# Attention masks added to the scores by eight 64x64 identity products on TensorE's quarters instead of four 128x128 ones

## The chip, the cores and the metric

One core of one Trainium2 chip runs the whole program. The metric is device time in microseconds (us) of one execution, as the median of several runs. TensorE multiplies matrices (PE in the profile; PEld is its loading of weights, which overlaps the multiplying), VectorE is DVE, ScalarE is ACT, GpSimd is POOL, and SyncE (SP) issues most DMAs.

## What is computed

A batch of 32 sequences of 128 tokens, 128 channels wide, passes through attention, a mixture of experts, attention with rotary positions, and a second mixture of experts, each with a layer norm before it and a sum with its input after it. Both attentions have 16 heads of 8 channels and read 77 keys from a context of their own. The change touches only the masking of their scores:

```python
# first attention: one mask for all sequences (128 x 77), one of padding for each sequence (32 x 77)
scores = jnp.einsum('bqhd,bkhd->bhqk', q, k) * SCALE
scores = jnp.where(attn_mask[None, None, :, :], -jnp.inf, scores)
scores = jnp.where(key_padding_mask[:, None, None, :], -jnp.inf, scores)
attn = jax.nn.softmax(scores, axis=-1)
# second attention: a query sees the 65 keys up to its own position
idx = q_pos + jnp.arange(-64, 1)[None, :]
local_mask = (idx < 0) | (idx >= S_k)
```

## The kernel before

Each attention is a pipeline over the 32 sequences, written out by hand: every engine has its own list of instructions, and semaphores tie the lists together. For sequence k TensorE does, in this order: turn the output of sequence k-2 (L1373), make the scores of k (`scores`, L1318), turn the shifted scores of k-1 so that keys lie on partitions (L1348, L1351), turn rows (L1382 to L1388), multiply by the values of k-1 (L1365), and make projections and router logits (L1416 to L1424). VectorE takes the maximum of each head's scores (L1061), subtracts it (L1062), and between these does the layer norm's statistics, the router and the sums with the input. ScalarE takes the exponentials and copies PSUM banks (a bank is a part of the accumulators) to SBUF. GpSimd spreads the keys of later sequences ahead of time (`keys`, L551), prepares values and sends token rows to the experts with indirect DMAs (L620).

The scores of one sequence fill four banks of the tile `S`, one for each group g of four heads: 128 queries on the partitions, 4 x 77 = 308 columns. `scores` waits until the query projection has been taken (`products_taken` or `q_set`), until the keys are spread (`kexp_ready`), and until VectorE has read the scores before (`sub_done`). Then it issues four products of 32 rows by 128 columns in float32 (L1328), each on its own quarter of TensorE's rows and into its own bank. The profile shows two matmul records for each of them, as for every float32 product. Four products of the 128x128 identity in bf16 with the masks then add the masks into the same four banks (L1330). The mask is one 128x77 tile read four times over. The last of the four raises `s_ready`, on which L1061 waits.

The masks come from two places. In the first attention GpSimd adds, for each sequence, the common mask `negA` and that sequence's padding `negP` into a ring `bias_qk` of 13 slots (L561), ahead of TensorE by up to 13 sequences. `negA` is made once by VectorE (L1139) from bytes that SP loads (L438). In the second attention the mask is one tile `bandb`, copied once by GpSimd (L532) from the constants `cst`, while the experts of the first half still run. Those constants come in one load behind the first few (L2200), which SP issues before the moves of the values (L709) and the loads behind them.

Of the kernel before, what the change touches and what calls it, by code (L numbers as in the profile page):

```python
# [13 lines left out]
U8 = mybir.dt.uint8  # L14
# [36 lines left out]
C_QUARTER = 716  # L51
C_END = 730
# [10 lines left out]
WARM = 38  # L63
CHUNK_AT = ((0, 128), (488, 360))

def shape_constants():
# [5 lines left out]
    c[:, C_BAND:C_BAND + TK] = np.where((k < q - WINDOW) | (k > q), MASKED, 0.0)  # L73
    half = DH // 2
# [175 lines left out]
def attention(nc, st, layer, w):  # L250
# [43 lines left out]
    if rope:  # L294
# [6 lines left out]
        bandb = sb("bandb", [128, TK], BF16)  # L301
    else:
# [3 lines left out]
        bias_qk = sb("bias_qk", [128, KR, TK], BF16)  # L306
        am8 = sb("am8", [128, TK], U8)
        negA = sb("negA", [128, TK])
# [126 lines left out]
    def sync(sp):  # L435
        if not rope:
            sp.dma_start(pad8[:, 0:SOON], w["pad"][:, 0:SOON]).then_inc(masks_in, 16)
            sp.dma_start(am8[:, :], w["am"]).then_inc(masks_in, 16)  # L438
# [78 lines left out]
    def gpsimd(pool):  # L517
        steps = Steps(pool_step)
        zero = st["zero"]
        if not rope:  # L520

            nc.gpsimd.memset(mv[:, :, :, :], 1.0).then_inc(mv_set, 1)
            nc.gpsimd.memset(raw[:, 2 * G:3 * G, :, :], 0.0).then_inc(mv_set, 1)
            nc.gpsimd.memset(vm[:, :, :, :], 0.0)
            nc.gpsimd.memset(xn[:, :, 0:1], 1.0)
            nc.gpsimd.memset(onesb[:, :], 1.0).then_inc(mv_set, 1)
            pool.wait_ge(mv_set, 3)
            pool.wait_ge(st["cst_in"], 48)
        else:
            pool.wait_ge(consts_in, n_const)  # L530
            pool.wait_ge(st["consts_in"], st["n_consts"])
            nc.gpsimd.tensor_copy(bandb[:, :], cst[:, C_BAND:C_BAND + TK]).then_inc(masks_set, 1)  # L532
# [18 lines left out]
        def keys(n):  # L551
# [7 lines left out]
            if not rope:  # L559
                pool.wait_ge(masks_set, 1 if n < MOVED_FIRST else 3)  # L560
                steps.mark(nc.gpsimd.tensor_tensor(  # L561
                    bias_qk[:, n % KR, :], negA[:, :], negP[:, n * TK:(n + 1) * TK], ALU.add))
# [341 lines left out]
    def vector(dve):  # L904
# [232 lines left out]
        if not rope:  # L1137
            dve.wait_ge(masks_in, 48)
            V.tensor_scalar(negA[:, :], am8[:, :], MASKED, None, ALU.mult)  # L1139
# [177 lines left out]
    def tensor(pe):  # L1317
        def scores(n):  # L1318
# [6 lines left out]
            masks = bandb[:, :] if rope else bias_qk[:, n % KR, :]  # L1325
            for g in range(G):
                heads = slice(32 * g, 32 * g + 32)
                nc.tensor.matmul(S[:, g, 0:GK], qT[heads, n % 2, :], kexp[heads, n % KR, :, :], start=True, stop=False)  # L1328
            for g in range(G):
                last = nc.tensor.matmul(S[:, g, 0:GK], identb[:, :], masks.unsqueeze(1).broadcast_to([128, J, TK]),  # L1330
                                        start=False, stop=True)
# [117 lines left out]
        else:  # L1449
# [3 lines left out]
            pe.wait_ge(masks_set, 1)  # L1453
# [873 lines left out]
def layout(v):  # L2327
# [17 lines left out]
    out["a0_am"], out["a0_amT"], out["a0_pad"], out["a0_padT"] = mask, mask.T, np.repeat(pad.reshape(1, -1), 128, 0), pad.T  # L2345
# [44 lines left out]
```

## Time and profile before

| what | us |
|---|---|
| median of 3 runs | 703.93 |
| lowest and highest run | 702.35, 705.06 |
| span of the profiled execution | 699.0 |
| median less that span | 4.93 |
| TensorE busy in the span | 653.6 |
| VectorE busy | 527.0 |
| GpSimd busy | 507.5 |
| ScalarE busy | 421.3 |

The profiled execution's own time outside its span is not given by the profile, so the difference of 4.93 us between median and span stands for what lies around the span. The attentions fill about 14 to 190 us and 366 to 548 us of the span. TensorE's granted clock is at the full 2.4 GHz in nearly all of both; at half of it (1.2 GHz) only in a few short stretches, of which one covers the start of the second attention. Busy times of TensorE are modelled, and a busy engine isn't always the one that sets the pace: the chain of waits and the idle times of the other engines decide that.

### The profile page before, as it was taken

Reading aid. Unit: us, or ns where it says so; the run is one execution under the profiler, and the core shown is the slowest. Engines: PE = TensorE matmul, PEld = TensorE weight load, DVE = VectorE, ACT = ScalarE, POOL = GpSimd, SP = SyncE. Lnnn points to the kernel's source line nnn. Section 1 sums busy time; section 2 is a strip of 40 time slices with the busy share of each in tenths; the row PEclk is TensorE's granted clock in tenths of the full one; section 3 lists DMA queues with packets and bytes.
Section 4 is the critical chain, followed back from the end, with each engine's and each line's share of the span. In section 5 each row is a group of like instructions: output and inputs, shape, how many; then the busy total and the mean of one; then the engine's idle time right before and its main releaser. Section 6 shows DMA issues by size and latency. Waiting matters only on the chain.

```text
span 699.0 us, 20550 instructions
## 1 busy us (share of the span) xinstructions
PE 653.6 (94%) x6836; PEld 550.9 (79%) x6836; DVE 527.0 (75%) x1507; ACT 421.3 (60%) x1166; POOL 507.5 (73%) x844
## 2 busy tenths in 40 slices
PE   8899999999988999999988999999899787999998
PEld 6577777777766999999985777777676676999997
DVE  4589999999853566665445789999999578778876
ACT  5567777776545333333444667677674675777773
POOL 5865588668765898887767776888787776777671
PEclk9999999999989999999997999999999999999999
DMA  5490001011423332334311101011121013333375
GB/s 178 112 352 6 10 26 33 26 33 35 159 68 93 116 119 62 95 97 126 88 41 35 32 17 32 29 59 46 35 71 49 32 48 98 103 100 101 94 251 195
DMA packets 45404, 57.69 MB, mean 83 GB/s; under 512 B 11379, under 2 KB 37142, under 8 KB 44630
## 3 DMA queue, kind: packets, MB, share of 16 engines
q1 hardware_dynamic: 36086, 38.12, 18.4%
q0 software_dynamic: 8640, 17.97, 7.6%
q8 instruction: 58, 0.95, 0.6%
q10 hardware_dynamic: 576, 0.29, 0.2%
q14 instruction: 44, 0.36, 0.2%
HBM read 33.77 MB, written 22.08 MB: 80 GB/s over the span
## 4 chain that ended last, share of the span: by engine, by line
PE 38%; DVE 23%; POOL 20%; issue 11%; DMA 2%; ACT 2%; SPq 2%; DVEq 0%; POOLq 0%; ACTq 0%
POOL results L1624 10%; PE S L2059 6%; PE ptp L2078 6%; DVE mx L1061 5%; DVE pr L1062 5%; PE M L1365 4%; PE S L1328 4%; POOL rows L620 3%; PE ptp L1348 3%; PE S L1330 3%; POOL xi L1617 3%; PE M L1416 2%; PE S L2065 2%; PE ptp L1351 2%; SPq L709 1%
## 5 line engine op out<-in xcount | busy, mean ns | idle before, releaser
L620 POOL DMA_INDIRECT rows<-out_rows,posi x128 | 126.9, 991 | 48.5 <-issue 28.5
L803 ACT ACTIVATE pT<-ptp 128x512 f32<-128x512 f32 (+1 forms) x192 | 94.1, 524 | 79.4 <-PE ptp L1348 72.3
L1061 DVE TENSOR_REDUCE mx<-S 128x16 f32<-128x1232 f32 x64 | 91.2, 1425 | 16.4 <-PE S L1330 15.8
L1624 POOL DMA_INDIRECT results<-early,xi x71 | 74.8, 1053 | 31.3 <-DVE early L1688 24.1
L1062 DVE TENSOR_TENSOR pr<-S,mx 128x1232 f32<-128x1232 f32 x64 | 92.2, 1441 | 2.2
L1929 POOL DMA_INDIRECT results<-early,xs x71 | 69.2, 975 | 27.4 <-issue 17.1
L1714 PE MATMUL S<-early,w1s 128*128 128x128 f32 x568 | 77.6, 280 | 5.0 <-DVE w1s L1681 3.3
L1724 PE MATMUL S<-first_w,early 128*128 x568 | 75.6, 276 | 0.7 <-DVE early L1688 0.7
L1714 PEld LDWEIGHTS S<-early,w1s 128*128 128x128 f32 x568 | 70.3, 195 | 7.6 <-issue 6.1
L1660 ACT ACTIVATE early<-S 128x128 f32<-128x128 f32 x71 | 19.6, 276 | 84.3 <-PE S L1707 84.3
L1688 DVE TENSOR_SCALAR early<-S,xs 128x128 f32<-128x128 f32 x71 | 24.9, 350 | 60.0 <-PE S L1724 33.2
L1365 PE MATMUL M<-pT,vm 128*32 128x128 f32 (+1 forms) x2048 | 70.0, 277 | 0.0
L1724 PEld LDWEIGHTS S<-first_w,early 128*128 128x128 f32 x568 | 69.0, 192 | 1.2 <-issue 0.9
L1348 PE MATMUL ptp<-cst,pr 128*128 128x128 f32 x512 | 68.9, 279 | 0.1
L1348 PEld LDWEIGHTS ptp<-cst,pr 128*128 128x128 f32 x512 | 61.7, 145 | 2.8 <-DVE pr L1062 0.3
L1328 PE MATMUL S<-first_w,qT 32*128 32x308 f32 x512 | 52.3, 477 | 11.0 <-DVE pr L1062 3.5
L1365 PEld LDWEIGHTS M<-pT,vm 128*32 128x32 f32 (+1 forms) x2048 | 52.4, 110 | 12.1 <-issue 11.6
L2059 PE MATMUL S<-early,w1s 128*128 128x128 f32 x426 | 53.7, 276 | 3.7 <-DVE w1s L1982 3.7
L2078 PE MATMUL ptp<-W,kT 128*128 (+1 forms) x412 | 56.3, 278 | 0.0
L2059 PEld LDWEIGHTS S<-early,w1s 128*128 128x128 f32 x426 | 50.4, 192 | 4.3 <-issue 4.3
L2078 PEld LDWEIGHTS ptp<-W,kT 128*128 128x128 f32 x412 | 52.2, 194 | 0.6
L1681 DVE COPY w1s<-first_w 128x512 f32 x71 | 39.9, 562 | 12.7 <-PE S L1714 7.8
(222 smaller groups left out, 1556.5 us busy)
## 6 DMA issues: line engine op xcount, KB each, us to landing
xs<-rows SPq DMA_DIRECT2D x142, 66.0 KB, 1.8
first_w<-in_e_W SPq DMA_DIRECT2D x2, 2048.0 KB, 8.5
swap<-results SPq DMA_DIRECT2D x32, 128.0 KB
first_w<-results SPq DMA_DIRECT2D x6, 512.0 KB, 7.9
rows<-out_rows,posi POOLq DMA_INDIRECT x128, 2.3
x_res<-in_x SPq DMA_DIRECT2D x1, 1536.0 KB, 8.6
W1r<-in_e_W SPq DMA_DIRECT2D x1, 1536.0 KB, 10.9
out_x<-x_res SPq DMA_DIRECT2D x3, 512.0 KB, 3.8
```

The lines of the kernel that those rows point to most:

```text
L620: nc.gpsimd.indirect_dma_start(rows[:, :], bass.IndirectOffsetOnAxis(posi[:, k, n:n + 1], 0), out_rows[:, ring_slot(groups, n), k, :], Non ...
L803: nc.scalar.activation(pT[0:rows_of, G * r:G * r + count, :], ptp[q % 2][0:rows_of, 0:count, :], ACT.Exp, scale=SCALE)\
L1061: do(V.tensor_reduce(mx[:, :].rearrange("p (g j) -> p g j", g=G), sc, AX.X, ALU.max))
L1062: V.tensor_tensor(pr[:, n % 2, :, :].rearrange("p (g j) k -> p g j k", g=G), sc, mx[:, :].rearrange("p (g j) -> p g j", g=G).unsqueeze(3). ...
L1328: nc.tensor.matmul(S[:, g, 0:GK], qT[heads, n % 2, :], kexp[heads, n % KR, :, :], start=True, stop=False)
L1348: last = nc.tensor.transpose(ptp[q % 2][:, g, :], flat[:, g // 2, at:at + 128], ident)
L1365: last = nc.tensor.matmul(OT[32 * g:32 * g + 32, half * T:(half + 1) * T], vm[0:rows_of, n % 2, block + g, :], pT[0:rows_of, chunk, :], st ...
L1624: nc.gpsimd.indirect_dma_start(results[:, :], bass.IndirectOffsetOnAxis(xi[:, s:s + 1], 0), ys[:, s, :], None)\
L1714: last = nc.tensor.matmul(hTp[n % 2][:, c, :], w1s[:, n % 2, c * 128:(c + 1) * 128], xsT[:, n % 3, :], start=True, stop=True)
L1724: last = nc.tensor.matmul(yp, hT[:, n % 2, c, :], w2[:, c, :], start=(c == 0), stop=(c == FC - 1))
L2059: last = nc.tensor.matmul(out[:, at * 128:(at + 1) * 128], w1s[:, u % 2, at, c * 128:(c + 1) * 128], xsT[:, r % 3, at, :], start=True, sto ...
L2078: last = nc.tensor.matmul(yp(u)[:, at, :], hT[:, u % 2, c * 256 + at * 128:c * 256 + (at + 1) * 128], w2[:, c, :], start=(c == 0), stop=(c ...
```

## The change

The four full mask products of a sequence become eight of 64 rows by 64 columns. Each uses one of the four quarters of TensorE: the rows (partitions of identity and mask) are the lower or the upper 64, the columns (partitions of `S` that are written) too. Banks 0 and 2 take their masks from the two quarters on the diagonal, banks 1 and 3 from the other two. For those two the mask has to lie on the opposite half of the partitions, so every mask is kept twice, the second time with its two halves exchanged (`np.roll` by 64). That doubles `bandb`, `bias_qk`, `negA` and the bytes `am8`, adds 77 columns to the constants, a second copy on GpSimd in the second attention, and makes the sum L561 twice as wide. The score products now close their accumulation (`stop=True`), and the mask products add onto them. TensorE's second attention waits for both copies.

```diff
-C_QUARTER = 716
-C_END = 730
+C_SWAP = 716
+C_QUARTER = 793
+C_END = 807
+MASKS_AT = [(g + odd, rows_at, 64 - rows_at if odd else rows_at) for g in (0, 2) for odd in range(2) for rows_at in (0, 64)]
+    c[:, C_SWAP:C_SWAP + TK] = np.roll(c[:, C_BAND:C_BAND + TK], 64, 0)
-        bandb = sb("bandb", [128, TK], BF16)
+        bandb = sb("bandb", [128, 2, TK], BF16)
-        bias_qk = sb("bias_qk", [128, KR, TK], BF16)
-        am8 = sb("am8", [128, TK], U8)
-        negA = sb("negA", [128, TK])
+        bias_qk = sb("bias_qk", [128, KR, 2, TK], BF16)
+        am8 = sb("am8", [128, 2, TK], U8)
+        negA = sb("negA", [128, 2, TK])
-            nc.gpsimd.tensor_copy(bandb[:, :], cst[:, C_BAND:C_BAND + TK]).then_inc(masks_set, 1)
+            nc.gpsimd.tensor_copy(bandb[:, 0, :], cst[:, C_BAND:C_BAND + TK]).then_inc(masks_set, 1)
+            nc.gpsimd.tensor_copy(bandb[:, 1, :], cst[:, C_SWAP:C_SWAP + TK]).then_inc(masks_set, 1)
                 steps.mark(nc.gpsimd.tensor_tensor(
-                    bias_qk[:, n % KR, :], negA[:, :], negP[:, n * TK:(n + 1) * TK], ALU.add))
+                    bias_qk[:, n % KR, :, :], negA[:, :, :], negP[:, n * TK:(n + 1) * TK].unsqueeze(1).broadcast_to([128, 2, TK]), ALU.add))
-            V.tensor_scalar(negA[:, :], am8[:, :], MASKED, None, ALU.mult)
+            V.tensor_scalar(negA[:, :, :], am8[:, :, :], MASKED, None, ALU.mult)
-            masks = bandb[:, :] if rope else bias_qk[:, n % KR, :]
+            masks = bandb[:, :, :] if rope else bias_qk[:, n % KR, :, :]
             for g in range(G):
                 heads = slice(32 * g, 32 * g + 32)
-                nc.tensor.matmul(S[:, g, 0:GK], qT[heads, n % 2, :], kexp[heads, n % KR, :, :], start=True, stop=False)
-            for g in range(G):
-                last = nc.tensor.matmul(S[:, g, 0:GK], identb[:, :], masks.unsqueeze(1).broadcast_to([128, J, TK]),
-                                        start=False, stop=True)
+                nc.tensor.matmul(S[:, g, 0:GK], qT[heads, n % 2, :], kexp[heads, n % KR, :, :], start=True, stop=True,
+                                 skip_group_check=True)
+            for g, rows_at, q_at in MASKS_AT:
+                rows_of, q_of = slice(rows_at, rows_at + 64), slice(q_at, q_at + 64)
+                last = nc.tensor.matmul(S[q_of, g, 0:GK], identb[rows_of, rows_of],
+                                        masks[rows_of, int(rows_at != q_at), :].unsqueeze(1).broadcast_to([64, J, TK]),
+                                        start=False, stop=True, skip_group_check=True)
-            pe.wait_ge(masks_set, 1)
+            pe.wait_ge(masks_set, 2)
-    out["a0_am"], out["a0_amT"], out["a0_pad"], out["a0_padT"] = mask, mask.T, np.repeat(pad.reshape(1, -1), 128, 0), pad.T
+    out["a0_am"], out["a0_amT"], out["a0_pad"], out["a0_padT"] = np.stack([mask, np.roll(mask, 64, 0)], 1), mask.T, np.repeat(pad.reshape(1, -1), 128, 0), pad.T
```

## Rows read from the trace of the kernel before

**Rows 1.** The page: its span, and part 4, the chain that ended last.

```profile
span 699.0 us, 20550 instructions
...
PE 38%; DVE 23%; POOL 20%; issue 11%; DMA 2%; ACT 2%; SPq 2%; DVEq 0%; POOLq 0%; ACTq 0%
POOL results L1624 10%; PE S L2059 6%; PE ptp L2078 6%; DVE mx L1061 5%; DVE pr L1062 5%; PE M L1365 4%; PE S L1328 4%; POOL rows L620 3%; PE ptp L1348 3%; PE S L1330 3%; POOL xi L1617 3%; PE M L1416 2%; PE S L2065 2%; PE ptp L1351 2%; SPq L709 1%
```

**Rows 2.** Busy time by stretch: us, PE, PEld, DVE, ACT, POOL, clock, DMA share, GB/s.

```profile
32.00:64.00 32.00, 31.90 (x407) 23.85 (x404) 27.04 (x58) 22.48 (x66) 19.95 (x49) 1.00 0.61 231
64.00:98.00 34.00, 33.85 (x457) 25.49 (x457) 32.07 (x86) 25.76 (x74) 22.79 (x48) 1.00 0.04 14
98.00:142.00 44.00, 42.72 (x553) 32.29 (x550) 41.97 (x124) 31.47 (x91) 34.89 (x64) 1.00 0.09 28
142.00:190.00 48.00, 45.94 (x615) 34.46 (x617) 45.59 (x145) 31.39 (x84) 36.07 (x62) 1.00 0.21 71
366.00:396.00 30.00, 25.94 (x276) 18.49 (x277) 18.61 (x28) 15.32 (x44) 21.52 (x44) 0.83 0.11 33
396.00:450.00 54.00, 53.87 (x690) 41.04 (x693) 46.99 (x112) 39.41 (x123) 40.01 (x83) 1.00 0.10 29
450.00:548.00 98.00, 91.14 (x1162) 68.60 (x1154) 89.77 (x273) 61.76 (x184) 77.83 (x138) 0.98 0.17 49
```

**Rows 3.** Chains of the stretches, in order of time: start, us, what (groups of pieces).

```profile
32.13 0.64 PE S L1330 x4
32.77 0.87 PE ptp L1348 x8
...
77.50 0.67 PE S L1330 x4
...
78.19 1.45 DVE mx L1061
...
508.93 0.64 PE S L1330 x4
```

**Rows 4.** Timeline of one sequence's scores, narrow windows: start, us, engine, line, count.

```profile
92.30 0.20 PEld L1328 LDWEIGHTS S<-first_w,qT 32*128 32x128 f32 x4
...
92.19 0.54 PE L1328 MATMUL S<-first_w,qT 32*128 32x308 f32 x4
...
92.56 0.44 PE L1328 MATMUL S<-first_w,qT 32*128 32x308 f32 x4
...
92.92 0.10 PEld L1330 LDWEIGHTS S<-bias_qk,identb 128*128 128x128 bf16 x1 [0.42 <-issue]
...
93.08 0.57 PE L1330 MATMUL S<-bias_qk,identb 128*128 128x308 bf16 x3
...
93.49 0.27 PE L1348 MATMUL ptp<-cst,pr 128*128 128x128 f32 x1
```

**Rows 5.** Timeline of the value products on quarters of 32 columns, same sequence.

```profile
95.13 1.08 PE L1365 MATMUL M<-pT,vm 128*32 128x128 f32 x32
...
95.15 0.25 PEld L1365 LDWEIGHTS M<-pT,vm 128*32 128x32 f32 x9
```

**Rows 6.** The waits: weight loads before the masks in the run; VectorE from 98 to 142 us.

```profile
PEld S L1330 <- issue: 27.6, 64, 0.8
...
DVE mx L1061 <- PE S L1330: 0.3, 1, 0.3
```

**Rows 7.** Single lines that the change widens or repeats: ns min/median/max, first and last start.

```profile
L561 POOL TENSOR_TENSOR bias_qk<-negA,swap x32: 312/326/347, 9.1 to 121.4; 128x77 bf16<-128x77 f32 x32
...
L563 POOL TENSOR_TENSOR first_w<-kT,cst x64: 693/702/716, 9.3 to 450.2; 128x308 f32<-128x308 f32 x64
...
L1139 DVE TENSOR_SCALAR negA<-am x1: 202/202/202, 6.9 to 6.9; 128x77 f32<-128x77 uint8 x1
...
L532 POOL CAST bandb<-cst x1: 257/257/257, 333.9 to 333.9; 128x77 bf16<-128x77 f32 x1
```

**Rows 8.** DMA issues by line: count, KB each, us to landing.

```profile
cst<-in_cst SPq DMA_DIRECT2D x1, 275.0 KB, 6.0
```

More of the change, by code:

```diff
@@ L437, in sync @@
             sp.dma_start(pad8[:, 0:SOON], w["pad"][:, 0:SOON]).then_inc(masks_in, 16)
-            sp.dma_start(am8[:, :], w["am"]).then_inc(masks_in, 16)
+            sp.dma_start(am8[:, :, :], w["am"]).then_inc(masks_in, 16)
             sp.dma_start(ctxT[:, SOON:], st["ctxT_dram"][:, SOON:]).then_inc(ctx_in[1], 16)
```

## The prediction

> **What bounds the kernel now.** I read the page first. The chain that ended last spends 38% on TensorE, 23% on VectorE and 20% on GpSimd, and the mask products L1330 alone are 3% of the span of 699.0 us, some 21 us [rows 1]. The 64 blocks of 0.64 us are 41 us, so about half of them lie on the chain. So the second view was the busy time by stretch, to see who sets the pace where. From 32 to 64 and from 396 to 450 us TensorE has no idle time (31.90 of 32, 53.87 of 54) while VectorE has 5 and 7 us to spare. From 64 to 142 us VectorE is nearly as full as TensorE (32.07 of 34, 41.97 of 44), from 142 to 190 us it stays so, and from 450 to 548 us TensorE, VectorE and GpSimd are each idle for some of the 98 us (6.9, 8.2 and 20.2), so they wait for one another [rows 2]. The third view, the chain of each stretch in order of time, tells what a shorter mask block is worth. I counted the L1330 blocks on it, and what follows each [rows 3]: 32 of 64 blocks lie on it, from the one at 32.13 us to the one at 508.93 us. After 26 of them the chain stays on TensorE (as at 32.13, with the transposes L1348 behind), after 6 it goes over to VectorE's maximum (as at 77.50, with L1061 at 78.19). The 26 gain what the block gets shorter for TensorE, the 6 what `s_ready` comes earlier. By stretch (TensorE next, VectorE next): 32 to 64 us 7 and 0; 64 to 98 2 and 2; 98 to 142 3 and 2; 142 to 190 none; 366 to 396 4 and 1; 396 to 450 8 and 0; 450 to 548 2 and 1.
>
> **The block itself, now.** In the timeline of one sequence the weight load of the first mask product starts at 92.92 after an idle time of 0.42 that no semaphore ended ("issue"), and the matmul of L1348 starts at 93.49: the block is 0.57 us [rows 4]. Three products after the first one take (93.49 - 93.08) / 3 = 0.137 each; the first has 0.16. So 308 columns of bf16 stream in 0.137, and the load of a full identity hides but for some 0.02.
>
> What the idle 0.42 is matters most. The second half of the score products starts at 92.56. The two halves are 92.56 - 92.19 = 0.37 apart, of which 92.30 - 92.19 = 0.11 is the load of 128 columns (the second loads go out when the first are in), so 0.26 is streaming. The last score product has streamed by about 92.84 (0.02 for its place as fourth), and the mask load waits for another 0.08 to 0.09, and isn't pulled ahead of it, as the load of L1348 is under the mask products. 
> - Load of 64 columns. The nearest rows are 0.11 for 128 columns (above) and 95.15 - 95.13 = 0.02 to 0.03 for 32 [rows 4, 5]. By columns 64 lie at 0.055; bounds 0.03 and 0.11. The second four loads hide under the first four products, as in both those rows.
> - Streaming. Four row quarters run side by side in L1328, and four column quarters side by side in L1365, there into one bank: 32 products in 1.08 us, where L1348 takes 0.87 for eight with as many columns [rows 3 to 5]. So I take two rounds of four at 0.137, 0.27, and 0.02 for the places in the round.
> - The way out. The array is in quarters before and whole after, so what came for nothing now costs a drain, 0.09 as at 92.84, and an open load for L1348, between 0.03 and 0.11, taken as 0.07. Lower bound: nothing of the 0.16, if the load is pulled ahead as before. Upper bound: 0.20.
>
> Sum: 0.055 + 0.27 + 0.02 + 0.09 + 0.07 = 0.51 against 0.57: TensorE gains 0.06 a sequence, with bounds of a gain of 0.24 (0.03 + 0.27 + 0.02 = 0.32) and a loss of 0.05 (0.11 + 0.27 + 0.02 + 0.11 + 0.11 = 0.62). Halving the products is mostly paid back on the way out. For VectorE more is left: the last mask product starts 0.43 after the first load now (93.49 less one product, 93.35, against 92.92) and 0.055 + 0.137 + 0.02 = 0.21 after it then, so `s_ready` comes 0.22 earlier (bounds 0.16 and 0.24).
>
> The page TensorEngine Tiling (Array Packing) of the Trainium skill states, under Key Properties, that changing the tiling mode drains the engine. The way in shows it here, as an idle 0.42; no row shows the way out. By that rule the lower bound, and with it the first rival below, falls away.
>
> **Along the chain.** 32 to 64 us: 7 x 0.06 = 0.42. 64 to 98: 2 x 0.06 + 2 x 0.22 = 0.56, of the 1.9 that VectorE has free. 98 to 142: 3 x 0.06 + 2 x 0.22 = 0.62, but VectorE waits there for scores for only 0.3 in all [rows 6], and its list is the same, so 0.3. 142 to 190: VectorE is late, not TensorE; 0. 366 to 396: 4 x 0.06 + 0.22 = 0.46. 396 to 450: 8 x 0.06 = 0.48. 450 to 548: VectorE is busy for 89.77 of 98 and GpSimd for 77.83, with the scatters L620 in its queue [rows 2]; I count nothing there, and I take half of the 0.94 of the second attention as given back in it, because those scatters keep their own pace. That is 0.42 + 0.56 + 0.3 + 0.47 = 1.75.
>
> **What it adds.** L561 gets 154 columns for 77: GpSimd took 326 ns for 77 and 702 ns for 308 (L563), so 154 are at 0.45, 0.12 more (at most 0.33, doubled) [rows 7]. That is 4 us over 32 sequences on an engine with 11 to 12 us free from 32 to 64 and from 64 to 98 us each [rows 2], up to 13 sequences ahead; the sums end at 121.4 us, and the indirect DMAs queued behind them in GpSimd's list have that slack too. If it had none, 4 us would show. Cost 0. L1139 on VectorE is on the path of the start, before the first values are moved: between 0 and 0.20 more, taken as 0.1. The second copy of the band mask, 0.26, stands in GpSimd's queue at 334 us between indirect DMAs of the experts; GpSimd waits for VectorE behind it, so 0, at most 0.26. TensorE's wait for it is 30 us later: 0. The constants grow by 77 x 128 x 4 bytes = 38.5 KB of 275, at 6.0 us for all: at most 0.8 if they were alone on the path, taken as 0.1, since the value moves behind them on SP wait for VectorE [rows 7, 8]. Together 0.2.
>
> So 1.75 - 0.2 = 1.55 us. Off the profiled execution that is 699.0 - 1.55 = 697.45 of span; with the 4.93 between span and median, 702.4.
>
> **The rivals.**
> - *No way out to pay.* If the load of L1348 is pulled ahead out of the quarters, TensorE gains 0.24: 1.7 from 32 to 64, 1.0 from 64 to 98 (VectorE waits there, all told, no more than 1.0 to 1.9), 0.3, then half of 12 x 0.24 + 0.25 = 3.1, so 1.55, less 0.2: 4.35 us, 699.6. For it: L1348's load was hidden before. Against it: L1330's load wasn't, at the same kind of border, in any of 64 sequences [rows 4, 6].
> - *Two row halves in one bank take turns (slower).* Each bank now gets its lower and its upper queries from two different row halves. Nothing in the trace has that: L1328 gives each row quarter its own bank, and L1365's column quarters, which share one, all use the full rows. If such a pair can't write side by side, the eight run as first; second and third; fourth and fifth; sixth and seventh; eighth: five steps for two. The block is 0.055 + 0.69 + 0.02 + 0.16 = 0.92, 0.35 longer than now, and `s_ready` comes 0.19 later. On the chain 26 x 0.35 + 6 x 0.19 = 10.2; from 142 to 190 us TensorE has 2.1 free against 9 x 0.35 = 3.2, so 1.1 more, and 0.7 at the borders of other stretches: 12 us, 715.9. It decides from the first step beyond four: at four the block is no longer shorter. The same page of the Trainium skill, under Gotcha 1: PSUM Pressure, says that different row tiles can't use one PSUM bank at the same time; taken by the letter it gives this case. L1365 speaks against it in part: quarters that write other partitions of one bank run side by side.
> - *No two quarters run together.* Eight times 0.137: 0.76 longer a sequence, 64 x 0.76 = 49 less what TensorE has free in rows 2 outside the chain, some 12: 37 us, 741.
> - *The four small loads queue up.* 4 x 0.055 ahead of the first round: the block is 0.1 longer than now, `s_ready` 0.06 to 0.1 earlier: 26 x 0.1 less 6 x 0.08, 2.1 us, 706. Against it: four loads of L1328 go out within 0.02 [rows 4].
>
> **How the numbers follow.** Chances: the forecast 0.60, no way out to pay 0.14, turns in a bank 0.14, queued loads 0.08, none together 0.04. The likeliest is 702.4, its own range 700.5 to 705. The range of 8 in 10 takes in the first rival and the queued loads and leaves out the two slow ones (0.18): 698.8 to 707.5. About 0.5%, 3.5 us, is what a measurement of this kernel can tell from no change, below 700.4 or above 707.4. Faster: most of the first rival and a little of the forecast, 0.17. Slower: 0.19. Within: 0.64.
>
> **What would show it.** In the profile after: the weight loads before the masks still idle for about 0.4; four mask matmuls start within 0.03 and the next four 0.14 later; an idle time before the load of L1348 that wasn't there, and 0.50 from the first mask load to L1348. VectorE's waits for the scores nearly vanish between 64 and 142 us, L1061 and L1062 stay at 1.4 us, L561 is at 0.45. Two starts 0.14 apart within one four would show turns in a bank. The forecast is wrong if the way out costs nothing, or more than 0.22.

## The result, and the profile after

The changed kernel takes 700.17 us (median of 8 runs, 697.25 to 703.74) where the kernel before, on the same chip, takes 704.62 (8 runs, 701.84 to 707.39): a ratio of 0.9935, with a 95% interval of 0.9907 to 0.9963. Two repeats beside other kernels gave 698.62 and 697.41 us, ratios 0.9939 and 0.9943. So the kernel is 4.5 us faster by this first comparison, and somewhere between 2.6 and 6.6; the forecast was 1.55 us off the span, and 702.4.

The runs of one kernel differ by several microseconds, and most of that goes with the mean granted clock in each run's record: over 201 runs of all kernels of this study, a microsecond more at the lower clock (1.2 GHz) is 0.35 us more of time. Where "clock taken out" stands below, this straight line is taken off. Slow executions are left out: three of before (711, 741 and 2137 us) and one of the copies alone (709 us). For the three rows of the change together (32 runs, against 82 of before) it leaves -3.4 us, with a 95% interval of 0.4. The mean time at the lower clock is 28.4 us in these rows and 29.6 in before, no clear difference, so the gain isn't a matter of the clock.

First the page of the changed kernel: its span, the chain that ended last by engine, and two of the costliest groups (busy time, mean ns of one, idle time just before and what ended it).

```profile
span 697.7 us, 21063 instructions
...
PE 34%; POOL 23%; DVE 22%; issue 13%; DMA 3%; ACT 2%; SPq 2%; POOLq 0%; DVEq 0%; ACTq 0%
...
L1065 DVE TENSOR_REDUCE mx<-S 128x16 f32<-128x1232 f32 x64 | 91.1, 1424 | 11.8 <-PE S L1336 11.6
...
L1355 PEld LDWEIGHTS ptp<-cst,pr 128*128 128x128 f32 x512 | 57.1, 145 | 16.2 <-issue 15.8
```

The lines have moved: the scores L1328 are L1332, the masks L1330 are L1336, the transposes L1348 are L1355, the maximum L1061 is L1065, the sums L561 are L565. On the chain TensorE falls from 38% to 34% [rows 1]. The last line is the new one: the weight loads of the transposes now idle for 15.8 us that no semaphore ended, some 0.25 before each sequence's first.

The busy time by stretch, with the columns of [rows 2]:

```profile
32.00:64.00 32.00, 31.43 (x435) 21.92 (x435) 26.80 (x59) 23.16 (x73) 22.42 (x51) 1.00 0.65 241
64.00:98.00 34.00, 33.63 (x484) 24.50 (x486) 32.65 (x85) 25.91 (x74) 23.59 (x49) 1.00 0.05 15
98.00:142.00 44.00, 41.62 (x586) 29.61 (x586) 42.45 (x125) 31.96 (x92) 35.88 (x65) 1.00 0.08 26
396.00:450.00 54.00, 53.62 (x741) 38.97 (x738) 47.49 (x114) 39.49 (x122) 40.66 (x83) 1.00 0.10 29
450.00:548.00 98.00, 89.86 (x1224) 65.19 (x1223) 89.52 (x279) 62.50 (x185) 77.36 (x138) 0.98 0.17 50
```

From 64 to 142 us VectorE is fuller than before (32.65 and 42.45 us for 32.07 and 41.97) and TensorE less so, GpSimd is busy for 0.8 to 1.0 us more in each of the two stretches, and in the second attention TensorE is still full from 396 to 450 [rows 2].

Then one sequence's scores, in narrow windows of the timeline of TensorE and its weight loads, the counterpart of [rows 4] (a window shows what runs in it, so a count depends on where the window is set).

```profile
92.88 0.44 PE L1332 MATMUL S<-first_w,qT 32*128 32x308 f32 x4
...
93.24 0.11 PEld L1336 LDWEIGHTS S<-bias_qk,identb 64*64 64x64 bf16 x4 [0.42 <-issue]
...
93.24 0.33 PE L1336 MATMUL S<-bias_qk,identb 64*64 64x308 bf16 x4
...
93.40 0.31 PE L1336 MATMUL S<-bias_qk,identb 64*64 64x308 bf16 x4
...
93.64 0.20 PEld L1355 LDWEIGHTS ptp<-cst,pr 128*128 128x128 f32 x2 [0.25 <-issue]
...
93.70 0.14 PEld L1355 LDWEIGHTS ptp<-cst,pr 128*128 128x128 f32 x1
```

The second half of the scores starts at 92.88, the first mask load at 93.24, after the same idle 0.42 as before. Four mask products start together at 93.24, four more at 93.40; the first load of the transposes waits until 93.64, and when it is in, at 93.70, the next one goes out. From the first mask load to that point the block takes 0.46 us, where 0.57 stood before (92.92 to 93.49, where the transposes' first weights were already in) [rows 4]. The last mask product starts 0.18 after the first load, where it started 0.43 after it. The sequence of [rows 4] is one of the longer ones of before: over 61 blocks the median is 0.545 before and 0.456 after, so 0.09 is the gain of a typical sequence, and 0.11 that of the longer form.

### The profile page after: what moved, and what is told of

It is laid out like the page before. It is cut to its first block, busy times and chain, and to the rows that moved or that the text cites. A ratio compares the mean times of both kernels' runs of the same rounds, so it can differ in the third digit from the quotient of the medians.

```text
span 697.7 us, 21063 instructions
## 1 busy us (share of the span) xinstructions
PE 648.6 (93%) x7092; PEld 535.8 (77%) x7092; DVE 527.4 (76%) x1507; ACT 421.5 (60%) x1166; POOL 514.5 (74%) x845
## 4 chain that ended last, share of the span: by engine, by line
PE 34%; POOL 23%; DVE 22%; issue 13%; DMA 3%; ACT 2%; SPq 2%; POOLq 0%; DVEq 0%; ACTq 0%
POOL results L1631 9%; PE S L2066 6%; PE ptp L2085 6%; POOL rows L624 5%; DVE mx L1065 5%; DVE pr L1066 5%; PE M L1372 4%; PE ptp L1355 3%; PE S L1332 3%; POOL xi L1624 3%; POOL rstd L552 2%; PE S L1336 2%; PE S L2072 2%; SPq L713 1%; PE M L1423 1%
## 5 line engine op out<-in xcount | busy, mean ns | idle before, releaser
L1065 DVE TENSOR_REDUCE mx<-S 128x16 f32<-128x1232 f32 x64 | 91.1, 1424 | 11.8 <-PE S L1336 11.6
L1355 PE MATMUL ptp<-cst,pr 128*128 128x128 f32 x512 | 72.1, 285 | 0.1
L1355 PEld LDWEIGHTS ptp<-cst,pr 128*128 128x128 f32 x512 | 57.1, 145 | 16.2 <-issue 15.8
L1332 PE MATMUL S<-first_w,qT 32*128 32x308 f32 x512 | 53.1, 484 | 11.5 <-DVE pr L1066 4.2
```

What stands on the lines that cost most here:

```text
L1065: do(V.tensor_reduce(mx[:, :].rearrange("p (g j) -> p g j", g=G), sc, AX.X, ALU.max))
L1355: last = nc.tensor.transpose(ptp[q % 2][:, g, :], flat[:, g // 2, at:at + 128], ident)
```

## The experiments

Two theories of the change go through the expectations. **P**: the price per block, multiplied along the chain as the prediction did it, with the block that the trace of after shows (0.11 us for TensorE, 0.25 for the scores), is what the kernel gains; its rivals are that a good part is given back later, and that products in one bank or one quarter hold one another up. **G**: GpSimd's wider sums, priced at nothing, cost part of the first attention.

The traces are compared by the starts of VectorE's 64 maxima, one for each sequence. Two profiles of the kernel before (the second is the last experiment but one) show which stretches repeat: from maximum 4 to 12, 12 to 20, 20 to 31, 40 to 47 and 47 to 60 they agree within 0.11 us, so differences there are the kernel's. Elsewhere they don't: 1.2 us apart from 0 to 4, 0.5 from 31 to 32 (the experts lie between), 0.8 from 32 to 40 and from 60 to 63, and 3.2 after the last. The table gives each stretch less that of the first profile of before, in microseconds. The last column is the time that VectorE's gate operations (`oh`, `both`, `gap`, `pos`, `carry`, `out_rows`, `posk`, `posi`) take between maxima 12 and 20, the same operations in all.

| kernel | 4 to 12 | 12 to 20 | 20 to 31 | 40 to 47 | 47 to 60 | gate operations, 12 to 20 |
|---|---|---|---|---|---|---|
| before (the stretch itself) | 41.35 | 42.08 | 58.57 | 37.81 | 75.47 | 5.78 |
| before, again | +0.02 | +0.02 | -0.11 | +0.03 | +0.11 | 5.82 |
| the change | -0.49 | +0.65 | -0.42 | -0.68 | +0.35 | 7.31 |
| the change, second run | -0.82 | +0.50 | -0.31 | -0.71 | +0.28 | 7.16 |
| the change, third run | -0.82 | +0.56 | -0.31 | -0.70 | +0.28 | 7.22 |
| copies only | -0.01 | +0.98 | +0.01 | +0.01 | +0.03 | 6.84 |
| same quarter in a row | -0.75 | +0.52 | -0.31 | -0.65 | +0.22 | 7.06 |
| sixteen products | -0.71 | +2.14 | +1.11 | -1.00 | -0.16 | 8.89 |
| sixteen in the second only | -0.81 | +0.50 | -0.31 | -0.99 | -0.19 | 7.15 |
| one copy in the first | -0.82 | -0.33 | -0.34 | -0.69 | +0.35 | 6.17 |
| before, in two quarters | +1.14 | +0.57 | +0.03 | +0.76 | +0.70 | 5.76 |
| before, no masks | -2.67 | -0.40 | -0.51 | -1.88 | -0.81 | 6.52 |

### The change, again

No edit.

> The changed kernel once more, against the kernel before on the same chip. In the trace after, the mask block is 0.455 us from the first mask load to the first transpose (0.565 before), so TensorE gains 0.11 a sequence, and the last mask product starts 0.18 after the first load (0.43 before), so VectorE gets its scores 0.25 earlier. Theory P (the gain is the block's price along the chain, as in the prediction's sum, with these two numbers in the place of 0.06 and 0.22): 0.77 + 0.72 + 0.3 + half of 1.6, less 0.2 for what is added, 2.4 us faster. Rival N (the change also moves something outside the block, such as stretches of low clock): 4.5 us faster or more, and spans of single runs that differ by whole low-clock stretches. In the first profile the first scores came 1.1 us later than before; if that is the change's own cost at the start, it is there again.

698.62 us (12 runs), ratio 0.9939 (0.9907 to 0.9972): the gain repeats. The span is 697.6. With the clock taken out, the 3.4 us of the three rows lie between the 2.4 of theory P and the 4.5 of rival N, so neither number came; the clock, by which N would show, is no different. The first maximum is 1.57 us later than in the first profile of before, here again, but 0.07 in the third run of the change, so this isn't a cost of the change.

### The copies alone

The doubled masks are made and read as in the change, but four full products join them, from the first copy.

```diff
-            for g, rows_at, q_at in MASKS_AT:
...
+            for g in range(G):
+                last = nc.tensor.matmul(S[:, g, 0:GK], identb[:, :], masks[:, 0, :].unsqueeze(1).broadcast_to([128, J, TK]),
+                                        start=False, stop=True)
```

> The doubled masks (bytes, negA, the ring of sums, the band and the constants) with the four full products of the kernel before, which read the first copy only. Theory P: the added work costs 0.2 us, between 0 and 1; L561's sum takes 0.45 us for 0.33 and is hidden; the mask block is 0.565 us as before. Rival S (the copies delay the start): the first maximum on VectorE comes 1.1 us later than before and the whole kernel is 1 us slower. Rival N: this kernel is already faster than before by some 2 us, since what moves lies in the data and not in the products.

702.19 us, ratio 0.9982 (0.9952 to 1.0011), with the clock taken out -0.5 with an interval of 0.7: by the time alone no difference. The table shows one: nothing anywhere but +0.98 from 12 to 20, where the gate operations take 1.06 more. So the copies aren't free in that stretch, against the prediction. Whether this loss lasts to the end isn't shown: the interval of the time leaves out a whole microsecond more. The first maximum is 0.24 later, so the start isn't delayed by the 1.1 of rival S, and 2 us of rival N lie outside the interval too: the products, not the copies, are what makes the kernel faster.

### Quarters without exchanged halves

The kernel before, with each full product cut into the two quarters on the diagonal; there is one copy, and each bank is written by two row halves at once.

```diff
...
             for g in range(G):
-                last = nc.tensor.matmul(S[:, g, 0:GK], identb[:, :], masks.unsqueeze(1).broadcast_to([128, J, TK]),
-                                        start=False, stop=True)
+                for rows_at in (0, 64):
+                    half = slice(rows_at, rows_at + 64)
+                    last = nc.tensor.matmul(S[half, g, 0:GK], identb[half, half], masks[half, :].unsqueeze(1).broadcast_to([64, J, TK]),
+                                            start=False, stop=True, skip_group_check=True)
```

> The kernel before with its four mask products each cut into the two quarters on the diagonal (rows and columns 0 to 63, and 64 to 127), without any second copy. Each bank gets its two row halves at the same time. If such a pair runs side by side: four rounds, load 0.03, 4 x 0.13, 0.02, way out 0.15: 0.70 us, 0.13 longer than before for TensorE, scores for VectorE at the same time as before. Theory P (26 of 64 blocks pass on to TensorE): 26 x 0.13 and a little where TensorE becomes late, 4 us slower than before. If the pair takes turns in its bank: eight rounds, 1.2 us, some 35 us slower. Rival N (something other than the block's length moves the time): within 1 us of before.

708.72 us, ratio 1.0073 (1.0042 to 1.0105); with the clock taken out +5.0, with an interval of 0.7. One sequence's block in its timeline:

```profile
96.94 0.32 PE L1333 MATMUL S<-bias_qk,identb 64*64 64x308 bf16 x2
...
96.94 0.41 PEld L1333 LDWEIGHTS S<-bias_qk,identb 64*64 64x64 bf16 x8 [0.42 <-issue]
97.61 0.20 PEld L1351 LDWEIGHTS ptp<-cst,pr 128*128 128x128 f32 x2 [0.25 <-issue]
```

The two products of one bank start together at 96.94 and the way out begins 0.67 later: four rounds of 0.137 and a way out, not eight rounds. Two row halves that write the upper and the lower partitions of one bank don't take turns. And the block is 0.16 longer than before (0.67 and a load of 0.06, against 0.57), which the chain prices at some 4 to 5 us: P holds in the other direction too. The ways in and out are paid once for any number of rounds, so here quartering pays only when all four quarters are used.

### The same quarter in a row

The change, with its two products of one quarter next to each other in the list.

```diff
-MASKS_AT = [(g + odd, rows_at, 64 - rows_at if odd else rows_at) for g in (0, 2) for odd in range(2) for rows_at in (0, 64)]
+MASKS_AT = [(g + odd, rows_at, 64 - rows_at if odd else rows_at) for odd in range(2) for rows_at in (0, 64) for g in (0, 2)]
```

> The changed kernel with its eight mask products in another order: the two that use the same quarter follow each other, so that products in order can only overlap in pairs: five rounds of 0.13 in place of two. The block is 0.85 us by that, 0.28 longer than before, and the last product starts 0.55 after the first load, 0.12 later than before. Theory P (32 of 64 blocks on the chain, 26 with TensorE next, 6 with VectorE next, and 1.5 where TensorE becomes the late one): 26 x 0.28 + 6 x 0.12 + 1.5 + 0.2 = 9.7 us slower than before, 12 slower than the change. Rival N (2 us of the change's gain come from elsewhere): 7.5 slower than before. If a product needn't wait for the one before it in its quarter, as fast as the change.

698.55 us, ratio 0.9938 (0.9908 to 0.9968): the same as the change, and the expectation of a slower kernel is refuted; its last case, that a product needn't wait, came. Its timeline shows why:

```profile
93.36 0.32 PE L1336 MATMUL S<-bias_qk,identb 64*64 64x308 bf16 x1
...
93.36 0.34 PE L1336 MATMUL S<-bias_qk,identb 64*64 64x308 bf16 x4
...
93.53 0.30 PE L1336 MATMUL S<-bias_qk,identb 64*64 64x308 bf16 x2
93.76 0.33 PE L1355 MATMUL ptp<-cst,pr 128*128 128x128 f32 x1
```

Four products still start within 0.02, and the way out ends as early as in the change (93.76 is 0.40 after 93.36; the median block is 0.01 longer). In the trace's records the first four are 6.7 ns apart, where neighbours of the list are 3.3 ns apart in the change: by this spacing every second one starts, and the four between them start 0.14 to 0.16 later. A product whose quarter is taken doesn't hold up those behind it on other quarters.

### Sixteen products of 32x32

Sixteen quarters of a quarter in both attentions, one round: four copies of the masks, each turned by 32 queries. To fit, the ring of sums is shortened to 6 and the band's copies come ready-made with the constants.

```diff
-        bias_qk = sb("bias_qk", [128, KR, 2, TK], BF16)
+        bias_qk = sb("bias_qk", [128, BR, 4, TK], BF16)
...
+            for g in range(G):
+                for r in range(4):
+                    q = (r - g) % 4
+                    rows_of, q_of = slice(32 * r, 32 * r + 32), slice(32 * q, 32 * q + 32)
+                    last = nc.tensor.matmul(S[q_of, g, 0:GK], identb[rows_of, rows_of],
+                                            masks[rows_of, g, :].unsqueeze(1).broadcast_to([32, J, TK]),
```

> Masks by sixteen products of 32 rows by 32 columns, all sixteen sub-squares of the array at once, from four copies turned by 0, 32, 64 and 96 partitions (the ring of sums shortened to six sequences to fit, the copies of the band kept as bf16 bits in the constants, so that GpSimd copies nothing in the second attention). One round in place of two: load 0.015, 0.13 of streaming, 0.05 for sixteen places, 0.15 for the way out: block 0.35 us, TensorE gains 0.22 a sequence against before (0.11 more than the change), the last product starts 0.07 after the first load (0.36 earlier than before). Theory P: 1.5 + 1.0 + 0.3 + half of 3.0, less 0.4: 3.9 us faster than before, 1.5 faster than the change, provided that GpSimd's sums at 0.70 us (12 us more over the first attention than in the change's... 8 us) stay hidden. Rival N: no faster than the change.

700.75 us, ratio 0.9958 (0.9934 to 0.9982): slower than the change, by 2.0 with the clock taken out (-1.4 against -3.4).

```profile
91.82 0.35 PE L1354 MATMUL S<-bias_qk,identb 32*32 32x308 bf16 x16
...
91.82 0.14 PEld L1354 LDWEIGHTS S<-bias_qk,identb 32*32 32x32 bf16 x16 [0.42 <-issue]
92.10 0.42 PEld L1373 LDWEIGHTS ptp<-cst,pr 128*128 128x128 f32 x4
```

On TensorE it does what it should: sixteen products start within 0.05, four row groups in each bank, and the next block begins 0.28 after the first load where the change has 0.40. In the second attention the stretch from 40 to 47 gains 1.00 for 0.70. The first attention loses it again: +2.14 from 12 to 20 and +1.11 from 20 to 31. There the sums are 308 columns wide, and GpSimd takes 0.72 us for each:

```profile
L561 POOL TENSOR_TENSOR bias_qk<-negA,swap x32: 707/722/757, 8.9 to 169.6; 128x308 bf16<-128x308 bf16 x32
```

Two things differ here at once: the sums are longer, and the ring of 6 keeps them going to 169.6 us, where they end at 123.0 in the change. How much of the 1.11 from 20 to 31 is due to either isn't shown.

### One copy in the first attention

The change, with one copy of the masks in the first attention. Its off-diagonal products read that copy unexchanged, which gives the same scores here only because all queries of one sequence have the same mask.

```diff
-        bias_qk = sb("bias_qk", [128, KR, 2, TK], BF16)
+        bias_qk = sb("bias_qk", [128, KR, 1, TK], BF16)
...
-                                        masks[rows_of, int(rows_at != q_at), :].unsqueeze(1).broadcast_to([64, J, TK]),
+                                        masks[rows_of, int(rope and rows_at != q_at), :].unsqueeze(1).broadcast_to([64, J, TK]),
```

> The changed kernel, but the first attention keeps one copy of its masks: the products off the diagonal read it without the exchange, which gives the same sums only because all queries share one mask in these inputs. L561's sum is 77 columns wide again (0.33 us for 0.45), negA and its bytes too; the products are those of the change. Theory G (the wider sums on GpSimd cost about 1 us between the 12th and the 20th sequence, where GpSimd has no wait left: in the copies-only kernel the first maximum of sequence 20 comes 1.0 later against before than that of sequence 12): about 1 us faster than the change, 4.3 faster than before. Rival (the wider sums are hidden, as the prediction has it): as the change, 3.3 faster than before. By sequence: G has no loss between sequence 12 and 20; the rival has 0.5 to 1.0, as in the change's two profiles.

698.56 us, ratio 0.9942 (0.9915 to 0.9968), with the clock taken out -3.9 with an interval of 0.7: the time can't tell it from the change. The trace can: from 12 to 20 it gains 0.33 where the change loses 0.57, and the gate operations are at 6.17 for 7.2. G holds, with a size of 0.9 us for that stretch. What stretches them is seen in one place. In the changed kernel, VectorE and GpSimd beside each other:

```profile
123.52 0.18 DVE L1018 RECIPROCAL out_rows<-gap 128x4 f32<-128x4 f32 x1
123.74 0.76 DVE L1019 TENSOR_TENSOR out_rows<-gap,out_rows 128x4 f32<-128x4 f32 x1
...
122.97 0.48 POOL L565 TENSOR_TENSOR bias_qk<-negA,swap 128x154 bf16<-128x154 f32 x1
123.39 0.71 POOL L567 TENSOR_TENSOR first_w<-kT,cst 128x308 f32<-128x308 f32 x1
124.06 0.41 POOL L582 TENSOR_TENSOR vm<-raw,cst 128x128 f32<-128x128 f32 x1
```

And with one copy:

```profile
122.33 0.17 DVE L1019 TENSOR_TENSOR out_rows<-gap,out_rows 128x4 f32<-128x4 f32 x1
122.41 0.33 DVE L1021 TENSOR_TENSOR posk<-oh,pos 128x64 f32<-128x64 f32 x1
...
121.97 0.41 POOL L582 TENSOR_TENSOR vm<-raw,cst 128x128 f32<-128x128 f32 x1
122.33 0.32 POOL L586 TENSOR_TENSOR vm<-raw,cst 128x64 f32<-128x64 f32 x1
```

A product of four columns takes 0.17 or 0.76: where it falls into a row of GpSimd's operations, it ends with one of them, here at 124.50, just behind L582 (124.06 + 0.41). With one copy it comes as L582 ends (121.97 + 0.41) and isn't held. The sums push that row later, into the gate. The long product stands on the chain of waits of the changed kernel:

```profile
123.74 0.76 DVE out_rows L1019
```

The width of the sums isn't the only thing that stretches the gate: without masks, where VectorE comes earlier and the sums are as narrow as before, the operations take 0.74 more (6.52 for 5.78). With sixteen products the waiting is plainest: the sum L561 runs from 101.18 to 101.93, VectorE's L1033 for 0.40 until 101.97, and its L1035, 0.23 in the median of all 20, for 1.15.

```profile
101.57 0.40 DVE L1033 TENSOR_TENSOR out_rows<-gap,out_rows 128x4 f32<-128x4 f32 x1
101.89 1.15 DVE L1035 TENSOR_TENSOR posk<-oh,pos 128x64 f32<-128x64 f32 x1
...
101.18 0.75 POOL L561 TENSOR_TENSOR bias_qk<-negA,swap 128x308 bf16<-128x308 bf16 x1
101.88 0.70 POOL L576 TENSOR_TENSOR first_w<-kT,cst 128x308 f32<-128x308 f32 x1
102.55 0.40 POOL L591 TENSOR_TENSOR vm<-raw,cst 128x128 f32<-128x128 f32 x1
```

The reciprocal L1018, with one input, stays at 0.18. The Trainium skill's page SBUF — State Buffer, in the section "SBUF: two separate sides", describes this: VectorE's operations with two inputs from SBUF and GpSimd's share a pair of ports, which one holds for a whole instruction while the other waits; the rows of L1019 and L1035 agree. L1017, which adds a constant to one input, is stretched too: 0.37 at 123.12 in the changed kernel, from 0.16 at the least, and once, as L1013 in the kernel without masks, 1.08, until 120.68, just behind GpSimd's L578 at 120.64. So one input alone isn't what spares the reciprocal.

### No masks

The kernel before without its mask products, which leaves the masking out of the result.

```diff
-            for g in range(G):
-                last = nc.tensor.matmul(S[:, g, 0:GK], identb[:, :], masks.unsqueeze(1).broadcast_to([128, J, TK]),
-                                        start=False, stop=True)
...
```

> The kernel before without any mask product, in both attentions: the scores stay unmasked. What a mask block of no length at all would give, so the most that any change of it can. TensorE gains 0.57 less the way out of the four row quarters, 0.07, so 0.5 a sequence; VectorE gets its scores 0.65 earlier. Theory P along the chain, held by what VectorE has free: 3.5 from 32 to 64 us, 1.9 from 64 to 98, 0.3 from 98 to 142, nothing to 190, 2.7 from 366 to 396, 4.0 to 450, up to 1.5 behind: 12 to 14 us faster if nothing is given back, 9 if half of the second attention's gain is. If VectorE and GpSimd set the pace as soon as TensorE is a little faster: no more than 5.

691.26 us (6 runs), ratio 0.9843 (0.9797 to 0.9889), with the clock taken out -12.9 with an interval of 0.9. That is P's number without giving back; with half of the second attention given back 9 were expected. From 47 to 60 it gains another 0.81, and gives nothing back. But the table bears P out only in the sum: its five stretches hold 6.3 of the 12.9, and a sequence gains 0.33 from 4 to 12 and 0.27 from 40 to 47, where TensorE was to gain 0.5. From 12 to 20 it gains 0.40, little more than one copy in the first attention does.

### Sixteen products in the second attention only

The change in the first attention, the sixteen in the second, where the copies of the band are constants and cost GpSimd nothing.

```diff
-            for g, rows_at, q_at in MASKS_AT:
+            for g, r in [(g, r) for g in range(G) for r in range(4)] if rope else ():
...
+            for g, rows_at, q_at in () if rope else MASKS_AT:
```

> The changed kernel with sixteen products of 32 x 32 in the second attention alone (four copies of the band as bf16 bits in the constants, nothing on GpSimd); the first attention as in the change. The block in the second attention is 0.34 us for 0.455, the last product starts 0.07 after the first load for 0.18. Theory P: 12 x 0.11 + 0.11 = 1.4 more than the change in the second attention, 4.7 us faster than before if nothing is given back, 4.0 if half is. Rival: as the change, 3.3, because what GpSimd sends at the end sets its own pace.

698.39 us, ratio 0.9937 (0.9911 to 0.9963), with the clock taken out -4.2 with an interval of 0.7, against -3.4 and 0.4 for the change. The 0.8 between them is no more than the two intervals allow. In the table it is 0.8 too: -0.99 for -0.70 from 40 to 47 and -0.19 for +0.30 from 47 to 60. It is the fastest of these versions that can be used, by a margin that the trace shows and the time doesn't settle.

### The kernel before, again

No edit; timed like a changed one, as a zero for all comparisons.

> The kernel before, unchanged, timed as if it were a changed one, for a second profile of it and as a zero for the comparisons. Summed over the sequences of both attentions, the traces of the changed kernel give about 2.2 us (0.10 for each of the first 12 sequences, 0.33 from the 20th to the 31st, 0.097 for each of 15 in the second attention, less 0.5 given back between the 12th and the 20th and 0.3 after the 47th); the times say 3.3, with the scatter by the granted clock taken out. Theory Z (the way in which a kernel is compared gives every newly timed one about 1 us): this kernel reads 0.9985, 1 us below before. Theory R (the rest of the gain is real and lies outside those sequences): it reads 1.000 within 0.003. In its trace the starts of the maxima between the 4th and the 31st, and between the 40th and the 60th, stay within 0.1 us of the first profile's; VectorE's gate operations between the 12th and the 20th maximum sum to 5.8 us as before, if theory G (GpSimd's wider sums stretch them) holds, and their sum doesn't differ by more than 0.3.

704.53 us, ratio 1.0009 (0.9976 to 1.0042), with the clock taken out +0.1 with an interval of 0.7. So the comparison itself gives a kernel nothing (theory R, not Z; the interval of the ratio alone would still hold Z's 0.9985), and the gate operations repeat: 5.82 us.

### The change, a third time

No edit.

> The change once more beside it. Theory R: 0.9950 with the scatter of some 0.003, the same 3 us below before. Theory Z: the same number, but then e9 is 1 us low too, and the change is worth 2.2. In the trace 0.8 us earlier from the 4th to the 12th maximum, 0.5 later from the 12th to the 20th, gate operations there 7.0 to 7.3 us.

697.41 us, ratio 0.9943 (0.9913 to 0.9973). In the trace the expected 0.8, 0.5 and 7.2 all came.

## Why the prediction was right, and where its sum was off

The direction was right, and the time lay in the range, but the forecast gain of 1.55 us was less than half of the measured 3.4 (by 0.4). By the time alone the first rival would be nearer: 700.17 is below the forecast's own range of 700.5 to 705, beside the 699.6 of *no way out to pay*, and times below 700.4 had a chance of 0.17. The trace decides: the way out is paid for, and no rival took the forecast's place. Two prices of the sum were wrong, in opposite directions, and that they partly cancel is luck. Step by step:

- **The way in** is as read: the loads before the masks still idle, 28.0 us over 64 sequences in the waits of the changed kernel (`PEld S L1336 <- issue`), 27.6 before [rows 6].

```profile
PEld S L1336 <- issue: 28.0, 64, 0.8
...
PEld ptp L1355 <- issue: 15.8, 61, 0.5
```

- **The way out** costs a drain and an open load, as forecast, and the first rival falls: the second of these lines is new, 15.8 us in 61 sequences. In the sequence shown the first load of L1355 goes out at 93.64 and has to be in before anything else, at 93.70.
- **The block** is the term of the sum that was too dear: 0.46 us and not 0.51, so TensorE gains 0.11 a sequence where 0.06 was forecast (0.09 in a typical one). The load of 64 columns was taken at 0.055, by columns between 0.11 for 128 and 0.02 to 0.03 for 32; the records show 0.028. Both rows it was taken from are float32 loads (L1328, L1365), and the new one is bf16. The open load of the transposes was taken at 0.07 and is 0.057, and the places in the round 0.01 less than taken. The second four start 0.13 to 0.16 after the first four, so the streaming was right. `s_ready` is 0.25 earlier, for 0.22.
- **Turns in a bank**, the rival on the slow side, would show four or more steps: there are two in the change, four in the kernel with two quarters, one with sixteen products. The Trainium skill's page TensorEngine Tiling (Array Packing), under Gotcha 1: PSUM Pressure, excludes row tiles that use one bank at the same time; for tiles that write different partitions of a bank these three runs show otherwise. Queued loads and quarters that can't run together fall with the same rows: four loads are 3.3 ns apart.
- **Along the chain** the multiplication held in the two stretches where TensorE sets the pace and the starts repeat. With 0.11 and 0.25, the prediction's own count of blocks gives 0.77 from 32 to 64 us, 0.72 to 98, 0.3 to 142, 0.69 from 366 to 396 and 0.88 to 450: 3.36 us. The table has 0.10 a sequence from 4 to 12 in two of three runs (0.82 / 8), and 0.10 from 40 to 47 in all three (0.70 / 7). That 3.36 meets the 3.4 of the times is luck in part: the count has a gain from 98 to 142 us where the table has a loss from 12 to 20, and it leaves out what is given back. Without masks 0.5 a sequence was expected and 0.33 and 0.27 came: TensorE itself falls idle there, for 0.9 us from 4 to 12 and 2.2 from 40 to 47 (0.0 and 0.1 before), so the price of a block can't be multiplied without end.
- **"Half given back"** in the second attention isn't settled. From 47 to 60 the change loses 0.28 to 0.35. That is nearly half of the 0.70 read from 40 to 47, and a fifth of 1.5, if the 8 sequences from 32 to 40, whose starts don't repeat, are counted at 0.10 too. That the scatters are what holds it there isn't shown: TensorE waits there for GpSimd's `qT` for 1.7 us (1.2 before) and for VectorE's `an` for 2.9 (2.2), and without masks nothing comes back.
- **The cost of the sums at nothing** is the second step that failed, in the other direction. Their own time was forecast well (0.45; the trace has 0.47). What the prediction didn't look for is what a longer operation of GpSimd does to VectorE. From maximum 12 to 20 the gate operations take 1.3 to 1.5 us more, and VectorE sets the pace there (42.45 busy of 44 us), so this comes off one for one: 8 x 0.10 gained less 1.45 is 0.65 lost, and the change loses 0.50 to 0.65. The same account gives -0.4 for one copy (measured -0.33), +1.1 for the copies alone (+0.98) and +2.0 for sixteen products (8 x 0.14 against 3.1; +2.14). It doesn't hold for the kernel without masks (a gain of 0.40, where 0.33 a sequence less 0.74 would be 1.9), so the 0.10 in it can't be TensorE's price alone: VectorE's idle time in the stretch falls from 1.95 us to 1.34 in the change and only to 1.28 without masks.
- **The start**, 0.2, can't be read: the first maximum comes between 0.07 and 1.57 later than in the first profile of before, among the five kernels with the loads of the change, and 0.60 later in the second profile of before.
- **Around the span**: 4.93 us were added between the span and the median. In the profiled runs since, the time is 1.8 us above the span (697.7 and 699.53; 701.9 and 703.71). The other 3.1 were scatter of the profiled execution. That did the forecast no harm: the 4.93 that is taken off with the span is added again, so 702.4 is the median of before less 1.55.

Added up by what repeats: 12 sequences at 0.10, less 0.57, 0.35 from 20 to 31, 15 sequences at 0.10, less 0.30 is 2.2 us. Of these, 0.9 are read in stretches that repeat (means of the three runs); the rest is 0.10 carried over to the 12 sequences from 0 to 4 and from 32 to 40. The times say 3.4 by 0.4. About 1 us of the gain therefore lies where the traces scatter by more than that (the experts between the attentions, and the end), and its place stays open: the zero run excludes that the comparison makes it. The copies alone have a gap of the same sign (+1.0 in the table, -0.5 by 0.7 in the time), so a part of what is lost from 12 to 20 may be won back later; no run settles it.

## What to carry to other kernels

Price a smaller tile by its whole block, with the way in and the way out: here quartering a full product pays when it fills all quarters (0.09 to 0.11 us a sequence), and loses with half of them (0.16). Before an operation that is "off the path" gets a price of nothing, see which operations of VectorE run beside it: GpSimd's 0.14 us more a sequence went with 1.4 us more of VectorE's gate operations in eight sequences, of which products as small as four columns waited behind it. How much of that reaches the end of the kernel isn't shown. And take a zero run and the stretches that repeat between two profiles of the same kernel, before a difference of some tenths is read from a trace.

## What the runs showed of the hardware that was not expected

- TensorE doesn't hold products in the order of the list when their quarter is taken: with the same quarter twice in a row, every second product started (by their spacing, 6.7 ns for 3.3), and the four that waited followed 0.14 to 0.16 us later. The Trainium skill's page TensorE: Matmul & The Clock Gate, under Part 3: Packing small matmuls — row/col tiling, states a strict order of the matmuls; this run shows otherwise for products on different quarters.
- Row groups that write different partitions of one bank accumulate side by side, up to four in each of four banks (sixteen products within 0.05 us).
- A 64-column load of bf16 takes as long as a 32-column load of float32: 0.028 us between the starts of two loads into one quarter (L1336 of the change, L1365 of before).
- VectorE's products with two inputs from SBUF, 0.16 to 0.19 us at their shortest, took up to 1.15 us beside a row of GpSimd's operations, while the reciprocal kept its 0.18. L1017, which adds a constant to one input, took 0.16 to 0.37 in the change.
